# TensorE's loop over pairs of batch groups in the fused stage, written out straight with constant addresses and counts

## What is computed

```
qn, kn, vn = layer_norm(query), layer_norm(key), layer_norm(value)    # key, value: the context
Q, K, V = qn @ wq + bq, kn @ wk + bk, vn @ wv + bv                     # 16 heads of 8
attn = softmax(einsum('bqhd,bkhd->bhqk', Q, K) / sqrt(8))
x = query + einsum('bhqk,bkhd->bqhd', attn, V) @ wo + bo
return x + gelu(layer_norm(x) @ w1 + b1) @ w2 + b2
```

## Time and profile before

| | us |
|---|---|
| median of three runs | 1424.19 (1421.41 to 1428.18) |
| the profiled execution | 1414.8 |
| its span, as the profile has it | 1413.0 |
| fused stage, TensorE's steps 0 to 17 | about 958 to 1283 of the span |
| mean granted TensorE clock of the whole span | 0.954 |

### The profile page before, as it was taken

One profiled execution on the slowest core, in us unless ns is written; L12 is line 12 of the kernel. 1 busy time (PEld: TensorE's weight loads), 2 busy tenths in 40 slices (PEclk: granted clock), 3 DMA queues, 4 the chain that ended last, 5 costly groups with the idle time before them and its releaser, 6 DMA issues. The chain is left out here.

```text
span 1413.0 us, 62179 instructions
## 1 busy us (share of the span) xinstructions
PE 1257.7 (89%) x24154; PEld 1044.5 (74%) x24154; DVE 906.9 (64%) x2232; ACT 952.2 (67%) x2004; POOL 877.3 (62%) x1416
## 2 busy tenths in 40 slices
PE   4999999989999998769999999886887777888997
PEld 2778877777878887649999999754665565665775
DVE  3888888877888785684555555446776666753331
ACT  1777777777888886167788766436776567755553
POOL 2577777776767763119999998567775566213331
PEclk9999999999999998599999999996998889999999
DMA  4233333332222220322222222342222222201221
GB/s 124 77 113 114 124 106 110 114 92 90 80 86 82 86 64 18 92 53 63 69 66 66 65 70 66 85 153 70 72 73 64 71 63 66 63 26 57 71 67 45
DMA packets 138036, 110.66 MB, mean 78 GB/s; under 512 B 16928, under 2 KB 113696, under 8 KB 137888
## 3 DMA queue, kind: packets, MB, share of 16 engines
q1 hardware_dynamic: 129440, 91.22, 21.6%
q0 software_dynamic: 8448, 17.32, 4.7%
HBM read 74.35 MB, written 34.08 MB: 77 GB/s over the span
## 5 line engine op out<-in xcount | busy, mean ns | idle before, releaser
L907 DVE TENSOR_REDUCE at_mx<-at_ps_s 128x16 f32<-128x1024 f32 x128 | 156.0, 1220 | 88.2 <-PE at_ps_s L594 44.7
L813 ACT ACTIVATE at_pt<-at_ps_t 128x1024 f32<-128x1024 f32 x128 | 130.5, 1020 | 52.5 <-PE at_ps_t L608 51.8
L2403 POOL DMA_INDIRECT ex_xg<-x,ex_ti x136 | 145.8, 1072 | 23.5 <-issue 21.9
L806 ACT ACTIVATE at_pr<-at_dd 128x1024 f32<-128x1024 f32 x128 | 135.2, 1056 | 34.6 <-DVE at_dd L915 34.6
L2475 ACT ACTIVATE ex_hg<-ex_ps_h,ex_wt 128x128 f32<-128x128 f32 x544 | 154.6, 374 | 1.2 <-PE ex_ps_y L2434 1.2
L2517 DVE COPY ex_wt<-experts 128x1156 f32 x133 | 103.3, 777 | 80.4 <-DVE ex_y L2523 74.4
L915 DVE TENSOR_TENSOR at_dd<-at_ps_s,at_mx 128x1024 f32<-128x1024 f32 x128 | 153.7, 1202 | 0.1
L2066 POOL DMA_INDIRECT l_yg<-rows,l_sl x128 | 125.7, 982 | 36.4 <-issue 35.6
L2425 PE MATMUL ex_ps_h<-ex_xt,ex_wt 128*128 128x128 f32 x1088 | 146.4, 278 | 0.9 <-ACT ex_xt L2467 0.8
L2434 PE MATMUL ex_ps_y<-ex_wt,ex_hg 128*128 128x128 f32 x1088 | 143.7, 275 | 0.4 <-ACT ex_hg L2475 0.4
L608 PE MATMUL at_ps_t<-ident,at_pr 128*128 128x128 f32 x1024 | 139.2, 279 | 5.4 <-issue 4.6
(11 more groups left out here) (276 smaller groups left out, 3236.2 us busy)
## 6 DMA issues: line engine op xcount, KB each, us to landing
rows<-ex_y SPq DMA_DIRECT2D x136, 64.0 KB
x<-at_ln_out SPq DMA_DIRECT2D x32, 256.0 KB, 3.1
at_kx<-in_xt SPq DMA_DIRECT2D x16, 256.0 KB, 2.6
at_qx<-in_xt SPq DMA_DIRECT2D x16, 256.0 KB, 2.6
at_vin<-in_xt SPq DMA_DIRECT2D x16, 256.0 KB, 2.6
at_xr<-in_x SPq DMA_DIRECT2D x16, 256.0 KB, 3.1
cx<-in_ctx SPq DMA_DIRECT2D x16, 256.0 KB, 3.0
x1t<-at_xt SPq DMA_DIRECT2D x16, 256.0 KB, 3.4
```

The source lines that it names most:

```text
L806: act.activation(pr[:, p], dd[:, p], ACT.Exp, scale=SCALE).then_inc(p_ready, 1)
L813: act.activation(pt[:, 2 * h + p], ps_t[:, :, :, :], ACT.Copy).then_inc(pt_ready, 1)
L907: dve.tensor_reduce(mx[:, p], ps_s[:, :, 4 * p:4 * p + 4, :], AX.X, ALU.max).then_inc(mx_ready, 1)
L2403: pool.indirect_dma_start(out=xg[:, s, :], out_offset=None, in_=x_src, in_offset=bass.IndirectOffsetOnAxis(ap=ti[:, s:s + 1], axis=0)).the ...
```

## The change

TensorE no longer calls `over_steps`. Python calls `step` for all groups with integer numbers, so steps 4 to 13 become straight instructions as steps 0 to 3 already were. The other four engines keep their loops, and no arithmetic, no buffer and no semaphore count changes.

```
                 for g in range(NG):
                     project_k(g)
                     project_v(g)
-                over_steps(pe, step, NG - 2)
+                for g in range(-4, NG + 2):
+                    step(At(1, g))
                 final.pe_part(pe, False)
```

## The result

The changed kernel takes 1383.03 us (median of 4 runs, 1381.56 to 1388.74) against 1422.8 us before (4 runs, 1417.95 to 1428.18): a ratio of 0.9727, 95% interval 0.968 to 0.9774. A second measurement with more runs gave 1382.42 us against 1416.0 (17 runs of before), ratio 0.9761, 0.9733 to 0.9788. The profiled execution fell from 1414.8 to 1381.56 us, its span from 1413.0 to 1379.8.

The account below looks back on a forecast made before the run. The prediction took PE, with its idle gaps and slow clock, as the bound. Four pairs at 35.65 us in place of 165.33 us save 22.7 us: 1424.2 − 22.7 = 1401.5 us, range 1390 to 1411.

Parts of the forecast that it names:

- The jumps: TensorE's four taken jumps in steps 6 to 13: 6.1 us each from whole steps, 24.4 us together.
- The straight pair: Two steps without a jump, from steps 2 to 5: 35.65 us, against 41.33 with a jump; 22.7 us saved over four.
- late blocks: Instruction blocks arriving late in straight code, mostly in `values` (L1617): 6.2 us in steps 0 to 5, counted within 35.65.
- The register arithmetic: PE's sequencer arithmetic in ten steps: taken as no gain, 0.7 us at most.
- The cover: Other engines in steps 3 and 4: POOL, nearest to late, needs about 29.8 us a pair, well under 35.65.
- The median's distance: Whole kernel: the median of runs lies 9.4 us above the profiled execution, and that distance was kept.
- The straight code streams without the late blocks: Rival for steps 6 to 13: every step takes 16.5 us, gain 33.3 us, time 1391 us; chance 0.05.
- The slower rival: All 16 `values` of steps 6 to 13 wait 3.0 us: 38 us more, time 1440 us; chance 0.04.

Follow-up runs that it names:

- held run: The changed kernel with six satisfied sequencer waits ahead of every even step from 4 on, making two steps exactly seven instruction blocks: 1393.81 us, ratio 0.9797.
- the hint: The kernel before, with one instruction at the head of TensorE's loop body announcing the jump at its end: 1376.66 us, then 1373.08 us with more runs.
- single-turn loops: The changed kernel with each pair of steps from 4 to 13 as a loop run once, register arithmetic kept, no jump taken: 1387.81 us, ratio 0.9775.

## Why the prediction was wrong

**The jumps: right, and a little short.** The prediction took 6.1 us a jump from whole steps. With the pause held at the place that it has in the loop (ahead of the 181st product there, the 180th here), no jump leaves 139.53 us, four jumps 165.33: 25.8 us, 6.4 a jump, or 6.8 without the 1.4 us that the held run's own six waits cost. That its price is a fetch of the target is shown by the hint.

**The straight pair: the step that failed.** The sum stood on 35.65 us a pair "as long as later steps are no unluckier than steps 2 to 4". They were much luckier: 132.64 / 4 = 33.16, and 33.76 in the second profile. The prediction counted the late blocks as scatter of the code's length. They have an exact place, 256 instructions apart. In the loop each turn starts at the same place, so the pause came at the end of `values` every time; steps 2 to 5, which I took as the measure, shared that place; straight on, it walks off by 6 instructions a pair.

This is 4 × 2.49 = 10.0 us (7.6 by the second profile), and it has two parts. The smaller is idle time: PE's waits without a releaser come to 9.5 us from step 5 to step 13, against 3.8 and 3.1 us in the two pairs that I used, 13.8 for four such pairs. The other is the clock. Both pairs ran at a granted clock of 0.95, the second in the earlier trace rows and the first in the line below, while the straight stretch had 0.99:

```profile
998.79:1034.40 35.61, 30.14 (x879) 23.96 (x879) 26.86 (x89) 27.48 (x56) 26.78 (x37) 0.95 0.28 80
```

If PE sets the pace, 0.05 of four pairs less 0.01 of the stretch is 5.8 us (an estimate); with the 4.3 us of idle time it makes up the 10.0. The prediction saw the lower clock behind the jumps and did not see that its straight pairs had a share of it too. The held run bears this out: with 14.8 us of idle time and a clock of 0.98 the same estimate gives 139.3 us, and it took 139.53. Its 6.9 us are therefore idle time for the most part, and the 3 us that it lacks to 142.6 are not shorter gaps but a better clock. Two gaps at the same place can differ by a microsecond because the fetch of the block starts and ends at other times; why its start varies is open.

**The register arithmetic: nothing, as said.** The single-turn loops show it, as far as two profiles of the changed kernel agree (2.4 us).

**The cover: as said.** PE's wait for POOL at L1626 over the stage is 1.5 us before and after; no engine took over.

**The median's distance: wrong.** I kept the profiled execution's 9.4 us under the median. With 17 runs before's median is 1416.0, 1.2 above its profiled execution. The changed kernel's median is 1.5 above its own. So the forecast's 18.5 us of error are 10.5 of the sum (33.2 measured in the profiles, 22.7 forecast) and 7.9 of this distance. By the larger sample the gain is 33.6 us, and the sum's error 10.9.

**The rivals.** "The straight code streams without the late blocks" had the right time to within 8 us (1391; steps of 16.5 us, measured mean 16.6), but only half its mechanism: the blocks still came, and the pauses with them, only shorter. The near hit is in part luck. I had given it 0.05, because I read the long steps 2 and 4 as two pieces of evidence when they shared one place. The rule of the Trainium skill's "Runtime: NRT & Kernel Launch", "Instruction fetch mechanics", that crossing a block is mostly hidden, holds for most of the 27 crossings between steps 5 and 13, but eight of them left PE idle for 0.66 to 2.04 us, and those of steps 2 and 4 for 3.01 and 2.36 us. The slower rival asked whether every `values` could meet the worst case; the held pause puts 4 of those 16 at the worst place, and it cost 4.5 to 6.9 us.

## What to carry to other kernels

This loop, whose body was fetched anew in every turn, paid twice: for the refill at the jump, and for late blocks that the loop pinned to one place, here a bad one. Look at the instruction queue's count per turn before anything else; if it is not zero, try a hint at the loop's head before writing the loop out, since here it beat the straight code and left the program as short as it was. And when a few steps serve as the measure for many, ask what is the same in them by accident, their clock included.

## What the runs showed of the hardware

- A hint on a body of some 1,800 PE instructions did not only make the jump cheap (4.708 to 0.221 us); from the second turn on no block was fetched. The Trainium skill's "Runtime: NRT & Kernel Launch", "Instruction fetch mechanics", gives PE's instruction memory 2048 instructions, which agrees with this; the kernel before, with the same body, fetched 9 blocks a turn. Why it does so without the hint was not tried.
- PE's long idle gaps without a releaser stand at multiples of 256 of its instructions: up to 3.0 us at the end of `values`, up to 1.7 us in the scores behind it, and under 0.2 us at 19 of the 27 block ends between steps 5 and 13. PE goes on 1.2 to 1.6 us after the block has landed. Little of this is hidden: at the eight gaps PE idled only 0.2 to 0.4 us less than its sequencer stood still.
- 100 satisfied waits in a row on PE's sequencer held PE back by 10.8 us (14.13 − 3.31), about 0.11 us each; in the trace they start 0.105 us apart.
